# Four attention layers on one core: one more key tile of each softmax sum moved from TensorE to GpSimd, the phases written out, and a new order of the side work

## The reference

```python
xg = xf.reshape(b, 32, c // 32, T); xn = (xg - mean) * rsqrt(var + eps)   # group norm, then scale and bias
qkv = einsum('oc,bct->bot', qkv_w, xn) + qkv_b
weight = softmax(einsum('bct,bcs->bts', q * scale, k * scale), axis=-1)    # 1024 x 1024 per head
a = einsum('bts,bcs->bct', weight, v)
h = einsum('oc,bct->bot', proj_w, a) + proj_b
```

## Time and profile before

| | |
|---|---|
| median of three runs | 1725.93 us (1725.8 to 1728.11) |
| the profiled execution, its own time | 1731.05 us |
| its span in the trace | 1729.3 us |
| phases 0 to 15 | from about 606 us to 1710 us of the span |
| mean granted TensorE clock | 0.958 of full |

### The profile page before, as it was taken

One profiled execution on the slowest core, in us unless ns is written; L12 is line 12 of the kernel. 1 busy time (PEld: TensorE's weight loads), 2 busy tenths in 40 slices (PEclk: granted clock), 3 DMA queues, 4 the chain that ended last, 5 costly groups with the idle time before them and its releaser, 6 DMA issues.

```text
span 1729.3 us, 25134 instructions
## 1 busy us (share of the span) xinstructions
PE 1595.8 (92%) x8238; PEld 1007.0 (58%) x8238; DVE 1052.1 (61%) x1664; ACT 898.7 (52%) x1488; POOL 992.4 (57%) x394
## 2 busy tenths in 40 slices
PE   4888969999997789999999999999999999999996
PEld 2776758888886455554555555555555455555532
DVE  3566645454551566676776676677677667667641
ACT  3444414343433165656666656666565565655652
POOL 2222303121222168697698687878868779759875
PEclk7999989999999689999999999999999999999998
DMA  4000000000000501130230321303303123032000
GB/s 151 19 19 19 1 1 1 1 1 1 19 1 10 137 8 42 33 74 14 62 74 2 74 49 44 74 4 71 80 1 75 41 60 74 6 95 64 12 25 25
DMA packets 31481, 67.58 MB, mean 39 GB/s; under 512 B 7472, under 2 KB 9328, under 8 KB 31344
## 3 DMA queue, kind: packets, MB, share of 16 engines
q1 hardware_dynamic: 31344, 65.82, 15.5%
HBM read 7.82 MB, written 4.19 MB: 7 GB/s over the span
## 4 chain that ended last, share of the span: by engine, by line
PE 40%; POOL 13%; issue 5%; SPq 4%; ACT 2%; DVE 2%; DMA 1%; POOLq 1%; ACTq 0%; DVEq 0%
POOL PA L1268 11%; PE psD L89 9%; PE psD L1023 9%; PE psO L957 8%; PE psA L1054 7%; PE psD L969 5%; PE psO L1054 3%; SPq L1300 2%; SPq L1298 2%; POOL SL L1251 1%; ACT PR L1226 1%; DVE BNS L1105 1%; PE psD L1017 1%; DMA QS<-SL 1%; ACTq L1177 0%
## 5 line engine op out<-in xcount | busy, mean ns | idle before, releaser
L1105 DVE TENSOR_REDUCE BNS<-psD 128x1 f32<-128x512 f32 x1024 | 644.2, 683 | 267.4 <-PE psD L1023 266.4
L1268 POOL TENSOR_TENSOR PA<-PA,PR 128x2048 f32<-128x2048 f32 x128 | 586.8, 4584 | 40.1 <-ACT PR L1226 29.7
L1226 ACT ACTIVATE PR<-psA 128x512 f32<-128x512 f32 x688 | 394.3, 602 | 319.9 <-PE psA L1054 276.2
L1023 PE MATMUL psD<-KS,QS 96*128 96x512 f32 x1024 | 425.6, 421 | 22.7 <-ACT SL L1191 13.1
L1054 PE MATMUL psA<-QS,KS 97*128 97x512 f32 x688 | 302.7, 442 | 22.6 <-ACT PR L1226 12.0
L680 POOL TENSOR_SCALAR P<-P,RS 128x1024 f32<-128x1024 f32 x64 | 72.0, 1126 | 361.1 <-DVE RS L398 361.1
L957 PE MATMUL psO<-PR,V 128*32 128x512 f32 x2048 | 257.8, 610 | 2.2 <-DVE A L1090 2.0
L1226 ACT ACTIVATE PR<-psO 128x512 f32<-128x512 f32 x336 | 202.3, 602 | 104.2 <-PE psO L1054 77.8
L1023 PEld LDWEIGHTS psD<-KS,QS 96*128 96x128 f32 x1024 | 201.1, 197 | 76.1 <-ACT SL L1191 15.8
L1268 POOL TENSOR_TENSOR PA<-PR 128x2048 f32<-128x2048 f32 x32 | 147.1, 4598 | 167.7 <-PE psD L969 143.3
L1054 PEld LDWEIGHTS psA<-QS,KS 97*128 97x128 f32 x688 | 132.1, 193 | 180.2 <-ACT PR L1226 113.2
(11 more groups left out here) (148 smaller groups left out, 2017.1 us busy)
## 6 DMA issues: line engine op xcount, KB each, us to landing
KS<-SH SPq DMA_DIRECT2D x128, 128.0 KB, 2.3
QS<-SH SPq DMA_DIRECT2D x128, 128.0 KB, 2.4
KS<-SL SPq DMA_DIRECT2D x64, 128.0 KB, 2.4
QS<-SL SPq DMA_DIRECT2D x64, 128.0 KB, 2.4
X<-x SPq DMA_DIRECT2D x4, 1024.0 KB, 7.3
out<-X SPq DMA_DIRECT2D x4, 1024.0 KB, 4.3
XN<-w SPq DMA_DIRECT2D x2, 768.0 KB, 7.7
KH<-KL SPq DMA_DIRECT2D x8, 128.0 KB, 2.3
```

The source lines that it names most:

```text
L1023: mm = e.matmul(full, QS[0:STACK, group, int(u == "a"), q, tile * PART:(tile + 1) * PART], KS[0:STACK, group, q, h * HALF:(h + 1) * HALF], ...
L1105: top = e.tensor_reduce(MXH[:, h, q, tile:tile + 1], full, AX.X, ALU.max)
L1226: e.activation(PR[:, J % 4, (s % QUADH) * HALF:(s % QUADH + 1) * HALF], score_bank(s, p), ACT.Exp, scale=scale).then_inc(exp_done, 1)
L1268: e.tensor_tensor(PA[:, :], PR[:, (J - 1) % 4, :] if j == 1 else PA[:, :], PR[:, J % 4, :], ALU.add).then_inc(sum_done, 1)
```

## The change

It does five things. DIRECT goes from 2 to 1, so ADDS is 6: GpSimd adds tiles 0 to 6 and TensorE's z takes PA and tile 7. In z, PA now comes first and its read is signalled by itself (`sums_read`); GpSimd's first add waits for that and not for the whole unit. ScalarE waits for single adds at tiles 0 to 2 of a phase and for unit z at tile 3 of a half. The `Fori` loops become Python loops. All tables of places are changed (EARLY is how many maxima tiles of a later group's second part are done ahead).

```diff
-DIRECT = 2
+DIRECT = 1
-        EARLY = 10
+        EARLY = 12
-        XN_AT = (32, 34, 36, 36)
-        BN_AT = (8.5, 10.5, 12.5, 14.5)
-        SIDE_AT = [{"v": (9, 13), "w": (21.5, 26), "K": (15.5, 31), "Q": (39.5, 41)},
-                   {"v": (8.5, 15), "w": (20, 27), "K": (41, 44), "Q": (46, 53), "p": (12.5, 28.5, 36, 56)}]
-        Z_AT = (39, 8)
+        XN_AT = (33, 34, 37, 38)
+        BN_AT = (11.5, 14.5, 15.5, 16.5)
+        SIDE_AT = [{"v": (9, 20), "w": (32, 56), "K": (38, 41.5), "Q": (43.5, 50.5)},
+                   {"v": (8, 9), "w": (15.5, 30.5), "K": (41, 43.5), "Q": (50.5, 56), "p": (33.5, 37, 12.2, 17.2)}]
+        Z_AT = (41, 7)
-        WEIGH = [(0, 11), (1, 11), (2, 17), (3, 17), (4, 23), (5, 28), (6, 34), (7, 34)]
+        WEIGH = [(0, 14), (1, 14), (2, 21), (3, 21), (4, 27), (5, 27), (6, 33), (7, 33)]
-            with e.Fori(0, B - 2) as r:
+            for r in range(B - 2):
-            with e.Fori(B, ROUNDS - 1) as r:
+            for r in range(B, ROUNDS - 1):
 # TensorE, sums():
-                        for j in (NT - 1, NT - 2, NT):
+                        for j in (NT, *range(NT - DIRECT, NT)):
...
-                                              start=(j == NT - 1), stop=(j == NT))
-                            if j == NT - 2:
+                                              start=(j == NT), stop=(j == NT - 1))
+                            if j == NT:
+                                mm.then_inc(sums_read, 1)
+                            elif j < NT - 1:
                                 mm.then_inc(av_done, 1)
 # ScalarE, before a key tile:
-                                wait(e, av_done, weighed(P, J - 4))
+                                if J % NT == 3:
+                                    if J >= NT or not (isinstance(P, int) and P == 0):
+                                        sums_of = [x[::2] for x in UNITS[place]].index(("z", 1 - J // NT))
+                                        e.wait_ge(d_full, base_of("all", place, r) + sums_of + 1)
+                                else:
+                                    wait(e, av_done, weighed(P, J - 4))
...
-                                    wait(e, sum_done, ADDS * 2 * P)
+                                    wait(e, sum_done, ADDS * 2 * P - max(ADDS - 4 - J, 0))
 # GpSimd, before the first add of a half:
-                                    before = [k for k, (u, _, i) in enumerate(UNITS[place]) if u == "z" and i == 1 - h][0]
-                                    e.wait_ge(d_full, base_of("all", place, r) + before + 1)
+                                    e.wait_ge(sums_read, 2 * P + h)
```

More of the change, by code:

```diff
@@ L929, in eight_heads_in @@
             st_full, exp_done = sem("scores_full" + n), sem("exp_done" + n)
+            sums_read = sem("sums_of_tiles_read" + n)
             av_done, sum_done, out_done = sem("av_done" + n), sem("sum_done" + n), sem("out_done" + n)
```

## The result

The changed kernel takes 1780.67 us (median of 5 runs, 1771.66 to 1781.59) against 1725.8 us beside it on the same chip (5 runs, 1720.05 to 1728.11): ratio 1.0315, interval 1.0293 to 1.0337. It is slower by 3.2%. Its profiled execution took 1771.66 us, the fastest of its five, with a span of 1769.8 us; the one before took 1731.05 us [the table of before], above every timed run of that kernel here. So the two profiles lie 40.5 us of span apart and the medians 54.9. Lines have moved: the adds are L1275 (L1268 before), the low parts L1259 (L1251), XL L1253 (L1245), z L970 (L969), the scores L1057 (L1054), the exponential L1234 (L1226).

The account below looks back on a forecast made before the run. The prediction took TensorE to bound the kernel before and GpSimd after. P = 0 +12.0, seven pairs +22.9, last phase -0.8 and tile 7's sum +1.0 gave +35.1 on 1725.93: 1761 us, 80% range 1716 to 1788.

Parts of the forecast that it names:

- the forecast's own case: GpSimd becomes the bound with waits at z and K: 141.4 us a pair, 1761 us in all, given 61%.
- TensorE is the bound before, GpSimd after: After the change GpSimd's chain is 134.3 us a pair before waits, TensorE's some 129, so the roles change.
- An add is 4.66 us: Each GpSimd tile add takes 4.66 us; four more a pair of phases cost 18.6 us.
- (1): From half 1's adds through the low parts to the next phase's adds, GpSimd does not wait.
- (2): Between the halves of phase A, GpSimd waits for TensorE's z to read PA: 1.3 to 2.2, taken 1.8 us.
- (3): Between the halves of phase B, after the second XL, GpSimd waits for K, then PA's read: 2.7 to 4.4, taken 4.4.
- (4): XN_AT puts four exponentials around ScalarE's second pair of activations, delaying the second XL 0 to 2.5 us, taken 0.9.
- the rest: At the end, tile 7's sum, done ahead before, now follows PA: +1.0 us.
- K does not stand in the way: Rival, 16%: GpSimd finds PA already read after the second XL; 136.0 us a pair, 1718 us, a little faster.
- TensorE still binds: Rival, 8% together with GpSimd flowing without a gap: 1703 us, or with shorter adds down to TensorE's 1682.
- The signs: Listed trace signs, among them GpSimd busy near 117 us a pair and a 3 to 5 us gap after the second XL.
- the loops: Three jumps back at 4.46 us each take 13.4 us off TensorE, buying nothing once GpSimd is the bound.

Follow-up runs that it names:

- experiment 3: The changed kernel with the sixth add taken back (five adds) and z of half 0 at 39: 1689.29 us, ratio 0.98 to the kernel before.
- experiment 12: The changed kernel with the output stores of blocks 0 to 2 moved behind the last one: 1781.82 us, ratio 1.0333 to the kernel before.
- experiment 1: The changed kernel with z of half 0 at 40.9 in place of 41, ahead of K in phases B: 1750.08 us, ratio 1.0153 to the kernel before.
- Experiment 7: The changed kernel with z ahead of K and the norm's four activations at 33, 34, 34, 34, not 33, 34, 37, 38: 1740.95 us.
- experiments 8 and 9: The changed kernel with each half's sixth add cut to 64 columns: 1705.71 us; the same with z ahead of K: 1671.64 us.
- experiment 6: The changed kernel with five adds, z of half 0 at 39 and the two Fori loops put back: 1707.34 us, ratio 0.9889 to the kernel before.
- experiment 2: The changed code (six adds, sums_read, written-out loops) with all tables of the kernel before: 1827.83 us, ratio 1.0605 to the kernel before.

## Why the prediction was right

The time came out in the forecast's own case. By its steps:

- *TensorE is the bound before, GpSimd after.* Right: the chain of waits above, and experiment 3, which gives TensorE its 69.77 of 70 us back by taking one add away.
- *An add is 4.66 us.* Mis-sized. In the first half shown above the six adds of a half take 975.76 to 1005.34 - 1.38 = 1003.96, 28.2 us: 4.70 each. Over 24 adds that is 1.0 us a pair more than predicted.
- *(1) No wait behind the low parts.* Right in P = 5 (971.07 + 4.73, next add at 975.76) and in every other phase.
- *(2) 1.8 us between the halves of kind A.* Right on the mean, by some luck: 1.38 in four phases, 1.67, 2.23 and 2.98 in the other three; mean 1.8. PA's read at full clock gives 1.38, below the 1.8 taken; the mean comes up to it through P = 11 and 13, where MROW was late (experiment 12), which the prediction did not have.
- *(3) 4.4 us behind the second XL.* Right in cause, by experiment 1, and near in size: 2.94 to 5.20 us, mean 4.0 in P = 2 to 14. The prediction took 2.19 us for K and 1.93 for PA's read. Measured, K takes 1.53 to 1.67 us in P = 2, 4, 8, 12 and 14 and 2.83 in P = 6 and 10; PA's read takes 1.93 or 1.94 in P = 4, 8, 10 and 12, 1.53 in P = 6 and 1.06 or 1.07 in P = 2 and 14. So the 4.0 is a mean of cases, after idle times of 2.7 to 3.0 us (6.3 in P = 6), and 4.4 came close to it as a sum of two terms of which neither held throughout. Its source had been read as one level, too: in the kernel before the granted clock fell at 1068.68, inside the K of P = 6 that began at 1068.10, so 2.19 is K partly at each level.
- *(4) 0.9 us on XL.* Nearly: from the factors to the end of the second XL it takes 936.29 + 2.34 - 927.92 = 10.7 us in P = 4 and 10.9 on the mean of P = 2 to 14, against the 9.9 + 0.9 predicted.

The pair, put together with the measured sizes: 24 x 4.70 + 9.5 (low parts) + 0.4 + 2.7 + 10.9 + 1.8 + 4.0 = 142.1. Measured, without the weight split, (1686.38 - 688.30 - 3.4) / 7 = 142.1; predicted 141.4. GpSimd's timeline at these two ends and in the last phase:

```profile
688.30 4.74 POOL L1259 TENSOR_TENSOR SL<-SL,SH 128x1024 fp32r<-128x1024 f32 x2
...
1686.38 4.73 POOL L1259 TENSOR_TENSOR SL<-SL,SH 128x1024 fp32r<-128x1024 f32 x2
...
1721.62 4.55 POOL L1275 TENSOR_TENSOR PA<-PR 128x2048 f32<-128x2048 f32 x1 [2.53 <-PE psD L970]
1726.32 23.27 POOL L1275 TENSOR_TENSOR PA<-PA,PR 128x2048 f32<-128x2048 f32 x5
```

The sum by profile: P = 0 ends 12.2 us later (predicted 12.0, with the earlier trace rows; its chain is 13.0 us longer, but its first add began at 612.96 and not at 613.76); the seven pairs take 998.1 against 970.3, +27.8 (22.9); the last phase 63.2, -0.1 (-0.8); the rest +0.6 (1.0). Together +40.5 against +35.1, and 4.9 of the 5.4 missing are in the pairs.

That the medians lie 54.9 us apart stays open by 14 us: each kernel's profiled execution stands at another place among its own runs, 5 us above the median before and 9 us below it after. By median the forecast of 1761 is 20 us low and inside its range.

What of the rivals: *K does not stand in the way* described the kernel before, and experiment 1 made it true; it gave 1750 and not 1718, a pair of 140.1 and not 136.0, since then XL ends later (the second one 11.3 us after the factors, not 9.9), an add is 4.70 us, and between the halves of kind A z is waited for 2.6 us and not 1.3. Experiment 7, which shortened that, found z waiting next. *TensorE still binds* came true only with the sixth add cut away (experiments 8 and 9). The signs came as listed, but for one figure: GpSimd is busy 59.69 + 66.58 = 126.3 us in a pair, not near 117. The prediction's own busy sum of 108.2 and four adds would have said 127.

Where the prediction was wrong in a part: it put the loops at 3 x 4.46 = 13.4 us off TensorE; under five adds they are 15 to 18 (experiment 6), 16.7 by the stretches from z to z, mostly because the idle times there are 3.07 to 3.56 us and not 2.25 to 2.53. And it put the single waits and K's new place at nothing. With six adds the old tables cost 47 us, so K's place was not free of GpSimd: a late exponential starves its adds. The single waits, which experiment 2 keeps, were never taken apart.

## What to carry to other kernels

- Before work is moved to an engine with busy time to spare, write down its chain in program order with every wait that it will have. Here 50.6 and 57.6 busy us of 70 looked like room for two adds of 4.7; with its fixed order and the waits of one pair it was 134 us of 139 after them, and the engine became the bound before it waited for anyone.
- Where two units have the same place in a hand-written order, look which comes first and what it waits for. A unit that frees another engine's buffer belongs ahead of one that waits for that engine: it was worth 30 us here (21 by profile), and 34 with cheap adds.
- Spread work in portions as large as the slack of each place: the same add was a loss in all halves (+61 us over five adds even with z ahead of K) and a gain in one of four (-11 us, of which some 5 belong to the add left out in the last half).

## What the runs showed of the hardware

A jump back of a register loop cost 5 to 6 us of timed run where TensorE binds (experiment 6 against 3): 3.07 to 3.56 us without an instruction, and then a stretch at the lower granted clock, in which 16 matmuls took 3.61 us and not 1.92. The Trainium skill ("Runtime: NRT & Kernel Launch", section "Instruction fetch mechanics") says that straight code is mostly fetched unseen and a jump out of the window is not. Experiments 3 and 6 agree, with 15 to 18 us for three jumps.

An idle time of 2.7 to 2.9 us on TensorE did not always bring the lower clock. In the changed kernel z's first 8 instructions behind it took 1.93 or 1.94 us in P = 4, 8 and 10 and 1.06 or 1.07 in P = 2 and 14.

An add of 128 x 2048 float32 by GpSimd takes 4.58 us on the mean of the changed kernel (4.49 to 4.62), and the next in a dependent row starts 4.70 to 4.73 us after it (medians of the kernels before and after). A cut to 64 columns takes 0.32 us.
